# Layer norm output transposed by DMA instead of TensorE, and the bias of V folded into the output bias

## Time and profile before

| | |
|---|---|
| runs of the kernel before | 2834.39 us median of 3 (2832.46 to 2834.86) |
| the profiled execution, first to last instruction | 2831.0 us |
| PE busy | 2758.9 us (97%) |
| DVE busy | 2113.9 us (75%) |
| ACT busy | 998.1 us (35%) |
| POOL busy | 711.4 us (25%) |
| DMA engines, mean share over the span | about 0.1, 92.61 MB moved |

### The profile page before, as it was taken

The page is one execution under the profiler, slowest core; times in us unless marked ns, Lnnn a source line. Parts: engine busy times, 40 slices in busy tenths (PEclk is TensorE's granted clock), DMA queues, the critical chain, the costliest instruction groups (busy, mean ns, idle before and its releaser), DMA issues.

```text
span 2831.0 us, 53917 instructions
## 1 busy us (share of the span) xinstructions
PE 2758.9 (97%) x22624; PEld 2046.0 (72%) x22624; DVE 2113.9 (75%) x3111; ACT 998.1 (35%) x1374; POOL 711.4 (25%) x537
## 2 busy tenths in 40 slices
PE   6999999999999999999999999999999999999995
PEld 4777777777777777777777777777777777777763
DVE  7777877777777777777777777778777777777777
ACT  5333333233333333333333332333332333332332
POOL 2122222122231222221222221222322222312223
PEclk9999999999999999999999999999999999999997
DMA  7000000000001000000000100000100000000000
GB/s 263 23 18 18 34 33 34 34 10 24 33 34 34 22 12 33 33 34 34 17 17 34 33 34 34 17 17 33 34 34 23 17 28 33 34 34 22 12 23 23
DMA packets 45917, 92.61 MB, mean 33 GB/s; under 512 B 11456, under 2 KB 20672, under 8 KB 45888
## 3 DMA queue, kind: packets, MB, share of 16 engines
q1 hardware_dynamic: 45888, 92.19, 9.5%
HBM read 67.02 MB, written 25.17 MB: 33 GB/s over the span
## 4 chain that ended last, share of the span: by engine, by line
PE 94%; DVE 4%; issue 1%; POOL 0%; DMA 0%; ACT 0%; POOLq 0%; SPq 0%; DVEq 0%; ACTq 0%
PE pair_prj L413 52%; PE pair_prj L423 26%; PE pair_att L437 5%; PE pair_prj L430 3%; PE pair_att L538 3%; PE pair_att L448 2%; PE pair_att L580 2%; PE pair_att L624 1%; DVE w_lo L698 0%; PE pair_att L602 0%; PE pair_att L600 0%; DMA arena<-in_L_gnn_Wq 0%; DVE arena L741 0%; DVE w_top L662 0%; DVE arena L780 0%
## 5 line engine op out<-in xcount | busy, mean ns | idle before, releaser
L413 PE MATMUL pair_prj<-w_hi,arena 128*128 128x512 f16 (+1 forms) x6144 | 1443.7, 326 | 0.0
L413 PE MATMUL pair_prj<-w_lo,arena 128*128 128x512 f16 (+1 forms) x3072 | 1001.0, 326 | 0.0
L413 PEld LDWEIGHTS pair_prj<-w_hi,arena 128*128 128x128 f16 x6144 | 602.6, 98 | 404.6 <-DVE arena L726 4.7
L423 PE MATMUL pair_prj<-arena,w_hi 128*128 128x256 f16 x4608 | 763.2, 273 | 9.4 <-DVE w_lo L698 9.2
L423 PE MATMUL pair_prj<-arena,w_lo 128*128 128x256 f16 x2304 | 628.8, 273 | 0.0
L423 PEld LDWEIGHTS pair_prj<-arena,w_hi 128*128 128x128 f16 x4608 | 449.1, 98 | 61.7 <-DVE w_lo L698 9.6
L413 PEld LDWEIGHTS pair_prj<-w_lo,arena 128*128 128x128 f16 x3072 | 300.8, 98 | 198.2 <-issue 0.3
L1314 POOL TENSOR_TENSOR rstd<-var_eps,minus_half 128x2 f32<-128x2 f32 x64 | 45.2, 706 | 930.9 <-DVE var_eps L718 930.9
L423 PEld LDWEIGHTS pair_prj<-arena,w_lo 128*128 128x128 f16 x2304 | 225.7, 98 | 26.5
L1346 POOL TENSOR_TENSOR arena<-arena 128x768 f32<-128x768 f32 x64 | 116.0, 1813 | 421.6 <-DVE arena L785 421.6
L1341 POOL TENSOR_TENSOR arena<-arena,b_row 128x768 f32<-128x768 f32 x64 | 116.6, 1822 | 375.7 <-DVE arena L763 375.7
(11 more groups left out here) (130 smaller groups left out, 3490.8 us busy)
## 6 DMA issues: line engine op xcount, KB each, us to landing
arena<-in_x SPq DMA_DIRECT2D x64, 768.0 KB, 4.3
out<-arena SPq DMA_DIRECT2D x64, 384.0 KB, 2.3
arena<-in_L_gnn_Wq SPq DMA_DIRECT2D x2, 1152.0 KB, 8.3
arena<-in_L_gnn_Wk SPq DMA_DIRECT2D x2, 1152.0 KB, 11.8
w_hi<-in_L_gnn_Wv SPq DMA_DIRECT2D x2, 1152.0 KB, 13.4
w_lo<-in_L_gnn_Wf SPq DMA_DIRECT2D x2, 1152.0 KB, 16.3
arena<-in_L_gnn_W SPq DMA_DIRECT2D x2, 1152.0 KB, 14.4
arena<-in_L_gnn_H_w SPq DMA_DIRECT2D x2, 1152.0 KB, 13.3
```

What stands on the lines that cost most here:

```text
L413: mm = nc.tensor.matmul(pair[:, lo:hi], lhs(a, k), weight(m, k, b)[:, lo:hi], start=(k == 0 and n == 0), stop=(k == KT - 1 and n == 2))
L423: mm = nc.tensor.matmul(pair[:, c * 256:(c + 1) * 256], weight(m, k, a)[:, o:o + P], (ht0_hi, ht0_lo)[b][:, k, :], start=(k == 0 and n == ...
```

## The change

- The normalised rows are written twice by ACT: first the fp16 high half into a new tile `h_hi`, then fp32 into `rows` (`relu_of_normal`, four instructions of 128x768 per layer and group where there were two). The copy from PSUM to the high half is gone.
- DVE subtracts in the row layout, SBUF to SBUF (`low_part`), into `h_lo`, which lies over the first half of each row of `rows`.
- SP issues `dma_start_transpose` of each 128x768 fp16 half into `ht*_hi` / `ht*_lo`: eight per step, four per layer. The ones of layer 1 stand behind the store of output block 0 and ahead of the load of the next `rows`, which now waits for them; the ones of layer 0 end SP's step. PE's 24 fp32 transposes per step are gone; its waits on `ht0_ready` / `ht1_ready` become waits on `ht_landed`, for both blocks and both halves at once. Group 0 of layer 0 is still transposed on PE.
- V has no `read_values`: ACT takes the high half from PSUM (`high_values`, scale VS), DVE the low half from PSUM (`low_values`), and `project_h(t)` waits for `v_ready` where it waited for `v_read`.
- Once, in step 0: DVE splits `bv` into fp16 halves, PE multiplies them by WF (`bias_of_values`, 36 matmuls), DVE adds the result to `bf_row`. PE's transposed probabilities of step 0, ACT's first `normalise(0)` and POOL's bias add of step 0 wait for that (`bf_folded`). One more small load (`bv_col`, 768 single values).

```diff
+def after_held(eng, held, sem, count):
+    if isinstance(count, int):
+        return after(eng, sem, count)
+    count = eng.snap(count)
+    eng.wait_ge(sem, count)
+    eng.sem_inc(held)
...
+        h_lo = rows.rearrange("p t c -> p (t c)").bitcast(F16).rearrange("p (t s c) -> p t s c", t=T, s=2)[:, :, 0, :]
+        LANDED = 2 * T * DMA
...
@@ SyncE (SP) @@
+            def transpose_rows(n, ht_hi, ht_lo, g):
+                after_held(sp, transposes_held, hi_made[n], 2 * g + 2 if n else 2 * g)
+                for t in range(T):
+                    sp.dma_start_transpose(ht_hi[:, :, t * P:(t + 1) * P], h_hi[:, t, :]).then_inc(ht_landed[n], DMA)
+                after_held(sp, transposes_held, lo_made[n], 2 * g + 2 if n else 2 * g)
+                for t in range(T):
+                    sp.dma_start_transpose(ht_lo[:, :, t * P:(t + 1) * P], h_lo[:, t, :]).then_inc(ht_landed[n], DMA)
...
+                if mid:
+                    if isinstance(j, int) and j == 0:
+                        sp.wait_ge(weight_ready, 2 * WG)
+                    else:
+                        after_held(sp, transposes_held, g_psum, 2 * j)
+                    transpose_rows(1, ht1_hi, ht1_lo, j)
                 if nxt and not first:
-                    after_alone(sp, eye_made, t0_psum, 2 * i + 2)
-                    if mid:
-                        after_alone(sp, eye_made, t1_psum, 2 * j + 2)
+                    after_alone(sp, eye_made, ht_landed[1], LANDED * (j + 1))
                     sp.dma_start(rows, x_g[i + 1]).then_inc(rows_loaded, DMA)
...
+                if nxt:
+                    after_held(sp, transposes_held, v_psum, 2 * i + 2)
+                    transpose_rows(0, ht0_hi, ht0_lo, i + 1)
...
@@ TensorE (PE) @@
                 def project_h(t):
-                    pe.wait_ge(ht1_ready, 2 * j + t + 1)
+                    pe.wait_ge(ht_landed[1], LANDED * (j + 1))
                     if now:
-                        pe.wait_ge(v_read, 2 * i + t + 1)
+                        pe.wait_ge(v_ready, 2 * i + t + 1)
...
-                    pe.wait_ge(ht0_ready, 2 * i + 2)
+                        pe.wait_ge(ht_landed[0], LANDED * i)
...
-                        transpose_rows(t, t1_psum)
...
-                next_rows(0)
                 context(0)
                 context(1)
-                next_rows(1)
...
@@ VectorE (DVE) @@
+            def low_part(n, t, g):
+                dve.wait_ge(full_made[n], g)
+                nc.vector.tensor_tensor(h_lo[:, t, :], rows[:, t, :], h_hi[:, t, :], ALU.subtract)\
+                    .then_inc(lo_made[n], 1)
...
-                    low_part_transposed(0, j, ht1_hi, ht1_lo, ht1_hi_ready, ht1_ready)
+                    low_part(1, 0, 2 * j + 1)
...
-                    read_values(0)
                     dve.wait_ge(exp0_ready, i + 1)
...
                     low_values(0)
-                    read_values(1)
                     low_values(1)
+                    if first:
+                        dve.wait_ge(bv_psum, 1)
+                        nc.vector.scalar_tensor_tensor(bf_row[:], pair_att[1][:, 0:C], col(w_undo, 6), bf_row[:],
+                                                       ALU.mult, ALU.add).then_inc(bf_folded, 1)
...
                 if nxt:
-                    low_part_transposed(0, i + 1, ht0_hi, ht0_lo, ht0_hi_ready, ht0_ready)
+                    low_part(0, 0, 2 * i + 1)
+                    low_part(0, 1, 2 * i + 2)
                 if now:
...
-                if nxt:
-                    low_part_transposed(1, i + 1, ht0_hi, ht0_lo, ht0_hi_ready, ht0_ready)
...
@@ ScalarE (ACT) @@
+            def normalise(n, src):
                 for t in range(T):
-                    nc.scalar.activation(rows[:, t, :], src[:, t, :], ACT.Relu, ...).then_inc(ready, 1)
+                    relu_of_normal(h_hi, n, src, t).then_inc(hi_made[n], 1)
+                for t in range(T):
+                    relu_of_normal(rows, n, src, t).then_inc(full_made[n], 1)
...
-                    act.wait_ge(t0_psum, 2 * i + 2 if now else 2 * GROUPS)
+                    act.wait_ge(ht_landed[0], LANDED * (i if now else GROUPS - 1))
...
                 if nxt and not first:
                     act.wait_ge(shift_ready[0], i + 2)
-                    normalise(0, rows, rows0_ready)
+                    act.wait_ge(ht_landed[1], LANDED * (j + 1))
+                    normalise(0, rows)
```

More of the change, by code:

```diff
@@ L231, in build_two_layer_gnn @@
         shift_ready = [sem(f"shift_ready{n}") for n in range(2)]
[L232 to L239, removed]
+        rows_first = sem("rows_first")
+        t_first = sem("t_first")
+        ht_first_hi = sem("ht_first_hi")
+        ht_first = sem("ht_first")
+        hi_made = [sem(f"hi_made{n}") for n in range(2)]
+        full_made = [sem(f"full_made{n}") for n in range(2)]
+        lo_made = [sem(f"lo_made{n}") for n in range(2)]
+        ht_landed = [sem(f"ht_landed{n}") for n in range(2)]
+        bv_split = sem("bv_split")
+        bv_psum = sem("bv_psum")
+        bf_folded = sem("bf_folded")
+        transposes_held = sem("transposes_held")
         q_psum = sem("q_psum")
@@ L362, in _ @@
             sp.dma_start(x1, x_g[0]).then_inc(x1_loaded, DMA)
-            for dst, src in ((bf_row, bf), (bv_row, bv), (bg_row, bg), (b1_row, b1)):
-                sp.dma_start(dst[:], src.partition_broadcast(P)).then_inc(const_loaded, DMA)
+            for dst, src in ((bf_row[:], bf), (bv_row, bv), (bg_row[:], bg), (b1_row[:], b1)):
+                sp.dma_start(dst, src.partition_broadcast(P)).then_inc(const_loaded, DMA)
+            with nc.allow_non_contiguous_dma(reason="one column of 768 values"):
+                sp.dma_start(bv_col[:], bv.rearrange("(k p) -> p k", p=P)).then_inc(const_loaded, DMA)
             for dst, src in ((src_row, w_src), (dst_row, w_dst)):
@@ L449, in attend1, with bias_of_values @@
                 mm.then_inc(o_psum, 1)
+            def bias_of_values():
+                pe.wait_ge(bv_split, 2)
+                pe.wait_ge(wf_ready, 2)
+                for lo, hi in ((0, 512), (512, C)):
+                    for k in range(KT):
+                        for n, (a, b) in enumerate(((0, 0), (0, 1), (1, 0))):
+                            mm = nc.tensor.matmul(pair_att[1][:, lo:hi], (bv_hi, bv_lo)[a][:, k, :],
+                                                  weight(WF, k, b)[:, lo:hi],
+                                                  start=(k == 0 and n == 0), stop=(k == KT - 1 and n == 2))
+                mm.then_inc(bv_psum, 1)
             pe.wait_ge(eye_made, 2)
             for t in range(T):
-                pe.wait_ge(rows0_ready, t + 1)
-                transpose_rows(t, t0_psum)
+                pe.wait_ge(rows_first, t + 1)
+                transpose_rows(t, t_first)
             def one(i, now, mid, last, nxt):
@@ L517, in one @@
                     attend1(1)
[L520 to L525, removed]
                 if now:
@@ L1130, in _ @@
             act.wait_ge(shift_ready[0], 1)
-            normalise(0, rows, rows0_ready)
             for t in range(T):
-                high_part_transposed(t, 0, t0_psum, ht0_hi, ht0_hi_ready)
+                relu_of_normal(rows, 0, rows, t).then_inc(rows_first, 1)
+            for t in range(T):
+                act.wait_ge(t_first, t + 1)
+                nc.scalar.activation(ht0_hi[:, :, t * P:(t + 1) * P],
+                                     pair_prj[t][:, 0:C].rearrange("p (k n) -> p k n", k=KT), ACT.Copy)\
+                    .then_inc(ht_first_hi, 1)
             for half in range(2):
@@ L1182, in one @@
                         act.wait_ge(weight_ready, 2 * WG)
-                    for t in range(T):
-                        high_part_transposed(t, j, t1_psum, ht1_hi, ht1_hi_ready)
                 if tail:
```

125 lines of the change are left out of this document (55 added, 70 removed).

## The result

| | before | after |
|---|---|---|
| median of the runs, us | 2833.43 (4 runs, 2832.46 to 2834.86) | 3202.99 (4 runs, 3200.9 to 3203.53) |
| ratio | | 1.1302 (95% 1.1286 to 1.1319) |
| span of the profiled execution, us | 2831.0 | 3200.9 |
| mean granted clock of PE | 0.99 | 0.946 |

The account below looks back on a forecast made before the run. PE was taken as the bound (97% busy), with DVE nearly as tight on two stretches. 29 periods x 3.6 = 104 us plus ends 27 gave 2831.0 + 131 = 2962, median 2965; own range 2920 to 3010, outer 2890 to 3260.

Parts of the forecast that it names:

- Part 4: SP's DMA transposes: 2.3 us each in series, hidden in the loop; they would cost only from 4.5 us each.
- rival A: DMA transposes slow, above 4.5 us each: 3160 us at 5.8 each, 3880 at 11.6; chance 0.22.
- Part 3: Doubled ACT normalise instructions delay later work: PE stalls 2.4 us at logit_operands, 1.0 at attend1(0), 0.5 at the context.
- Part 2: V without read_values: project_h(0) waits for low_values(0), a new PE stall of 2.5 us, starting 1.2 us later.
- Rival B: PE's granted clock falls below 1.00 in the loop; chance 0.10.
- Part 5: Steps outside the loop: 5.2 us in step 0, 1 in step 1, 2.2 in step 31, 19 in step 32.
- Part 1: PE's transposes removed: 2.66 us a period, 82 us over 31 periods if nothing else became late.
- rival C: Faster: PE stays the bound, new waits under the 2.66 us saved; period near 83 us, time 2780; chance 0.07.

Follow-up runs that it names:

- norm_last: Changed kernel with ACT's normalise moved behind its high halves of the probabilities, for both layers; 3112.69 us, ratio 1.0989.
- pool_narrow: Changed kernel with POOL's second pair of products (t = 1) on 8 of 768 columns, DVE's order untouched; 3079.55 us, ratio 1.0871.
- store_first: Changed kernel with SP's store of output block 1 ahead of the load of rows; 3151.95 us, ratio 1.1131.
- v_alone: Kernel before with only V's part of the change, bias of V left out, transposes still on PE; 2877.46 us, ratio 1.0159.
- filler: Changed kernel plus unread matmuls in PE's waits, 24 ahead of project_h(0) and 36 ahead of logit_operands; 3096.75 us, ratio 1.0931.
- all: Changed kernel with V's low half early, layer 0's low parts late, normalise behind ACT's high halves, step 32's transposes ahead of the store; 2764.87 us, ratio 0.9763.
- low_late: Changed kernel with layer 0's two low parts on DVE moved behind the attention terms; 3033.66 us, ratio 1.0686.

## Why the prediction came out at a third

**Part 4, transposes by DMA: right.** I took d = 2.3 us and called 4.5 the point from which they cost. A transposing DMA is issued every 1.28 us and lands 2.8 us after its issue, beside its neighbours; four have landed well ahead of PE, and rival A is dead. The 2.3 was an estimate by bytes from other transfers; the six 128x128 blocks of one instruction land together in 2.8. A pair of these instructions moves 151 GB/s, and the DMA engines are 80% busy meanwhile (the last two columns; the columns are those of the earlier trace rows):

```profile
1489.20:1491.80 2.60, 2.60 (x23) 2.04 (x22) 2.53 (x3) 0.00 (x0) 0.00 (x0) 1.00 0.80 151
```

Whether SP's issue or the transfer itself sets the 1.28 us is not shown.

**Part 3, four ACT instructions for two: places right, two of three sizes right.** attend1(0) waits 0.80 (1.0 forecast), the context 0.33 (0.5), and norm_last takes both away. logit_operands wait 4.93 where 2.4 were forecast. The step that failed is "Before, the same seven (in another order) stood between, and it took 8.82 us": they are not the same seven. The two low parts of the rows were reading PSUM and now read two SBUF tensors, and beside POOL's products they take 4.33 us for 1.82. pool_narrow gives 2.41, the size forecast, as soon as POOL is out of the way. The price stood in the trace of the kernel before, in DVE's timeline of step 0:

```profile
61.35 4.40 DVE L921 TENSOR_TENSOR p_place<-p_place,max 128x768 f32<-128x768 f32 x1
67.95 3.02 DVE L940 TENSOR_TENSOR p_place<-p_place,rinv 128x768 f32<-128x768 f32 x1
```

L940 is the product that takes 0.96 us in the earlier trace rows; here both stand beside POOL's long L1324, a row that I read for its end only.

**Part 2, V: mechanism right, size off.** 3.77 of stall on average where 2.5 were forecast. "None of these moves" failed: the product L966 takes 1.65 to 1.70 for 0.96, since POOL's copy now overlaps it, and that copy is late because the load of rows, issued behind the transposes, collides with the store that the copy waits for; POOL's L1369 is late by 0.64 through its turn with L752, and DVE's ELU behind it. store_first shows the first of these: 0.8 us of the stall goes. The rest, about 0.5, was not tried apart. v_alone, in which ACT, SP and the low parts are as before, has a stall of 1.43; with the 1.34 us of the 12 transposes that PE still does there that is 2.8, near the forecast.

**Rival B, the clock: wrong to hold it against the forecast.** I gave it 0.10 as another case, since the granted clock of 0.50 stood behind a stretch of 5.86 us without work on PE, and the stalls of 2.4 us that I forecast are shorter. It came on top: filler, which keeps the clock and moves nothing else forward, gets 3.7 us a period back, 106 of the 370. Two errors multiply here, for with the stalls as I sized them the clock might have been kept at project_h(0) (it was in store_first at 2.96) and sometimes at the gate rows (pool_narrow at 2.41).

**The sum.** A forecast period of +3.6 became +11.5: +1.3 at project_h(0), +2.5 at logit_operands, +3.4 by the clock, +0.8 by the loss of overlap at each break, which I had not counted at all, +0.3 of slower small matmuls, and -0.5 in the rest (attend1, context, scores, transposes). The outer range of 2890 to 3260 does hold 3203, but by the room that it left for rivals A and B and not by the forecast, whose own range ended at 3010. Two falls a period of 4.5 us each (an estimate: some 9 us at the 0.50 of the earlier trace rows) would have put 270 us of clock on the forecast's stalls: 3235, near 3203 by luck, for the clock was 106 on larger ones.

**Part 5, ends: 37 for 27.** Step 32 is +19.3 (19 forecast), by the wait for the DMA of 16.72, and "all" removes 15.9 of it with the order of SP. The place is right, the size in part luck: PE starts 7.3 us after add_h(0) ends where four landings of 2.3 were forecast, and the 36 matmuls behind the wait then take 8.80 for 6.86, which makes up for it. Step 0 is +8.9 for 5.2: the fold waits for DVE's L957, the high half of the bias, 4.89 us long beside POOL's split of the weights, where L959 of the same size behind it takes 1.02:

```profile
64.96 4.89 DVE L957 TENSOR_SCALAR arena<-bv_col,bv_scale 128x768 f16<-128x768 f32 x1
69.89 1.02 DVE L959 SCALAR_TENSOR_TENSOR arena<-bv_col,bv_scale,arena 128x768 f16<-128x768 f32 x1
```

It ends 0.42 us after POOL's L1352 does (69.43), so it looks held until that instruction is over; but it reads one wide SBUF tensor, not two, and whether this is the same taking of turns is open.

Step 31 is +5.9 for 2.2, 2.9 of it slow clock. Step 1 is +3 for 1.

**Part 1** is right: 3.05 us a period are gone with the gaps, and "all" shows them as a period of 83.23, near the 83 of rival C. Rival C came with three changes of order that the change didn't make; which of them it can do without was not tried.

**Open.** What decides whether the clock falls after a wait: the same 2.41 or 3.64 us did and did not lead to it (and, ahead of project_h(0) in step 31, 3.0 us led to 7.70 in the changed kernel and pool_narrow and to 6.01 in norm_last and store_first), so the length of one wait is not enough. For the same reason I can't say why the runs of low_late scatter over 24 us, nor why the gate rows alternate.

## What to carry to other kernels

Work taken off the bounding engine is a gain only if the others' lists are reordered with it: the same instructions gave +370 us in the order of the change and -68 with four of them changed. When an operand moves from PSUM to SBUF, re-price the instruction at every place where GpSimd works beside it (here 4.33 us for 1.82), and look in the whole trace, warm-up too, for the same form at another duration. When waits on TensorE are forecast, price them as wait, plus lost overlap, plus a slower clock behind them (here 9.96, 0.8 and 3.4 us a period), and not as rival cases.

## What the runs showed of the hardware

- DVE's instructions with two SBUF inputs took longer beside GpSimd instructions that read SBUF, and so did these, with ends as if the two took turns (after): the pair L752 4.33 us for 1.82 beside L1394 and L1395, L966 1.70 for 0.96 beside L1383, and GpSimd's L1395 2.52 and L1369 2.45 for 1.81. With GpSimd's second pair of products on 8 columns the pair L752 took 1.81 (pool_narrow). What the engines share is not shown. With one of the two inputs in PSUM neither was slowed (after, L849 at 1422.86, 0.96 us beside L1394, 1.80; before, the old low part L726 at 1406.88, 0.96 us beside L1341, 1.81).
- The transposing DMAs of 128x768 fp16, SBUF to SBUF (after): 1.28 us from issue to issue, 2.8 to landing, 151 GB/s in a pair at a DMA share of 0.80 (1489.2 to 1491.8). The load of rows and the store right behind them moved 269 GB/s at 0.71 (1492.6 to 1496.5).
- The load of rows (768 KB), issued 1.7 us ahead of the store of 384 KB, put the store's completion off by 1.0 us (POOL's wait 3.85 in after, 2.84 in store_first).
- The granted clock fell to 0.50 for some us behind idle stretches of 4.0 to 4.9 us ahead of logit_operands in every loop step (after, norm_last), behind 3.5 to 4.2 ahead of project_h(0) in 27 of 29 (after) but only 19 of 29 (norm_last), behind 2.41 in 9 of 29 (pool_narrow), and not behind 2.95 (store_first), 1.43 (v_alone) or 0.95 (low_late). 36 matmuls then took 7.2 to 8.8 us for 6.01.
- The idle break between two pieces of matmuls cost 0.16 us beside the idle time itself (v_alone: period +1.58 for a wait of 1.42).
